# A reordered turn in phase C, and one-hot rows of places that GpSimd makes and DRAM carries over to phase D

## What is computed

```python
x = x + jnp.tanh(g_xattn[2]) * _L2_xattn_ref(_layernorm(x), ctx_1024, ...)   # similarity attention
x = x + jnp.tanh(g_ffn[2])   * _L2_ffn_ref(_layernorm(x), ...)               # small feed-forward
x = x + jnp.tanh(g_xattn[3]) * _L3_xattn_ref(ctx_1024, ctx_1024, _layernorm(x), mask, ...)  # 16 heads of 16
x = x + jnp.tanh(g_ffn[3])   * _L3_ffn_ref(_layernorm(x), ...)               # 32 experts, top 4, and a shared one

def _L3_ffn_ref(x, router_w, router_bias, gate_w, up_w, down_w, sgate_w, sup_w, sdown_w):
    flat = x.reshape(B * T, D)
    scores = _softmax(flat @ router_w.T + router_bias)
    topk_scores, topk_idx = jax.lax.top_k(scores, 4)
    topk_scores = topk_scores / jnp.clip(topk_scores.sum(-1, keepdims=True), 1e-12, None)
    h = silu(einsum('nd,ehd->neh', flat, gate_w)) * einsum('nd,ehd->neh', flat, up_w)
    sel = take_along_axis(einsum('neh,edh->ned', h, down_w), topk_idx[:, :, None], axis=1)
    out = (sel * topk_scores[:, :, None]).sum(axis=1)
    return out + silu(flat @ sgate_w.T) * (flat @ sup_w.T) @ sdown_w.T
```

## Time and profile before

| | us |
|---|---|
| median of 3 runs | 4344.7 |
| profiled execution, whole | 4317.87 |
| its span, first to last instruction | 4316.1 |
| phase C, head attention's turns 0 to 15 | about 2983 to 3780 |
| phase C's last instruction | 3804.6 |
| phase D | 3806 to 4316 |
| a full turn of phase C | 50.55 |

### The profile page before, as it was taken

How to read it: one execution, slowest core, us unless ns; L and a number is a source line. 1 busy time by engine, 2 the same in 40 slices (tenths; PEclk the granted TensorE clock), 3 DMA queues, 4 the chain that set the end, 5 groups by cost and what they waited for, 6 DMA issues and landing times. The chain is left out here.

```text
span 4316.1 us, 78135 instructions
## 1 busy us (share of the span) xinstructions
PE 3976.5 (92%) x29168; PEld 2824.2 (65%) x29168; DVE 2323.2 (54%) x7158; ACT 1772.2 (41%) x3733; POOL 945.7 (22%) x1118
## 2 busy tenths in 40 slices
PE   7999999999999999999998899988999998769996
PEld 4666666666666666666665589966666666438963
DVE  4555655565556655665554522125566666474445
ACT  4455555555555455545542211113444444313420
POOL 2221222122212221222120011111000000005667
PEclk9999999999999999999999999999999999879998
DMA  3000000000000000000000169940000100029964
GB/s 114 1 4 9 8 6 4 9 8 6 3 9 8 6 4 9 8 6 4 6 13 33 74 237 333 332 165 13 30 23 26 31 21 11 13 71 299 335 200 143
DMA packets 136623, 284.25 MB, mean 66 GB/s; under 512 B 19968, under 2 KB 90176, under 8 KB 127680
## 3 DMA queue, kind: packets, MB, share of 16 engines
q1 hardware_dynamic: 84944, 200.03, 13.3%
q0 software_dynamic: 18336, 50.09, 4.0%
q10 hardware_dynamic: 32976, 29.13, 2.0%
HBM read 229.12 MB, written 50.07 MB: 65 GB/s over the span
## 5 line engine op out<-in xcount | busy, mean ns | idle before, releaser
L466 POOL TENSOR_SCALAR a_wide_p<-a_wide_p,a_w_inv 128x512 f32<-128x512 f32 x512 | 355.3, 706 | 1438.8 <-DVE a_w_inv L1133 1438.8
L903 ACT ACTIVATE a_wide_p<-a_wide_p,a_row_min 128x512 f32<-128x512 f32 x512 | 363.4, 713 | 114.0 <-DVE a_row_min L1128 112.5
L1203 DVE TENSOR_REDUCE a_q_pad<-ring 128x4 f32<-128x1024 f32 x256 | 301.1, 1219 | 87.5 <-PE ring L696 87.4
L1128 DVE CUSTOM_DVE_ANT_0 a_wide_p<-ring,a_neg_keys 128x512 f32<-128x512 f32 x403 | 266.0, 688 | 125.0 <-PE ring L550 124.8
L550 PE MATMUL ring<-a_qk 64*128 64x512 f32 x806 | 289.1, 643 | 21.6 <-DVE a_row_min L1128 15.0
L960 ACT ACTIVATE a_probs<-ring 128x1024 f32<-128x1024 f32 x256 | 250.5, 1019 | 72.6 <-PE ring L710 72.6
L1621 PE MATMUL ring<-b_xgt,b_we 128*128 128x128 f32 x2016 | 235.7, 275 | 0.5 <-DVE b_xgt L1784 0.5
L1621 PEld LDWEIGHTS ring<-b_xgt,b_we 128*128 128x128 f32 x2016 | 230.2, 192 | 1.1 <-DVE b_xgt L1784 0.7
L2689 DVE CUSTOM_DVE_ANT_0 c_junk<-ring,c_neg_mask 128x256 f32<-128x256 f32 x512 | 181.4, 420 | 89.3 <-PE ring L2219 89.3
L529 PE MATMUL acc<-a_kv_t,shared_w 128*128 128x512 f32 x392 | 196.0, 623 | 1.2 <-ACT a_kv_t L894 1.2
L1550 POOL DMA_INDIRECT d_xg<-d_rows,d_token_idx x159 | 150.1, 944 | 178.6 <-PE ring L1610 102.3
(11 more groups left out here) (464 smaller groups left out, 8547.3 us busy)
## 6 DMA issues: line engine op xcount, KB each, us to landing
b_we<-in_experts SPq DMA_DIRECT2D x63, 1536.0 KB, 9.3
d_we<-in_experts SPq DMA_DIRECT2D x159, 256.0 KB, 4.6
d_results<-d_yb ACTq DMA_DIRECT2D x159, 128.0 KB
b_results<-b_yb ACTq DMA_DIRECT2D x63, 128.0 KB, 9.0
a_cb<-in_ctx SPq DMA_DIRECT2D x16, 256.0 KB, 2.8
b_turned<-a_heads_t SPq DMA_DIRECT2D x16, 256.0 KB
b_rows<-a_heads SPq DMA_DIRECT2D x16, 256.0 KB
shared_x<-b_turned SPq DMA_DIRECT2D x8, 512.0 KB, 5.7
```

Source lines behind the costliest of these rows:

```text
L466: ins = pool.tensor_scalar(wide_p[:, h % 4, t, :], wide_p[:, h % 4, t, :], w_inv[:, t, h:h + 1], 1.0, ALU.mult, ALU.mult)
L903: ins = act.activation(wide_p[:, h % 4, t, :], wide_p[:, h % 4, t, :], ACT.Exp, scale=-1.0, bias=row_min[:, h, t:t + 1], accum_out=row_sum ...
L1128: dve.tensor_tensor_reduce(wide_p[:, h % 4, t, :], wbank(name), neg_keys[w % 2][:], -0.125, 3.0e38, ALU.add, ALU.min, row_min[:, h, t:t + ...
L1203: dve.tensor_reduce(q_pad[:, :, 2 * i:2 * i + 2, HD].rearrange("p t h -> p h t"), s, AX.X, ALU.max, negate=True).then_inc(nr.taken(name), 1)
```

## The change

It has four parts. (1) Phase C's turn is put in another order: TensorE turns c_x_e first, then c_o_t, then the queries; the logits come ahead of the first group of scores; f_out comes behind the second group, the projections n_project and f_project behind the fourth, and x_context behind the second queries. ScalarE follows and copies c_o_t's second half ahead of the last hidden copy. VectorE does n_values_in at the turn's head (with a wait for the values' last use), and e_apply, e_shares and route_choose ahead of x_products. (2) e_rank writes the places too: a rank's lower seven bits, as the starts of experts are whole multiples of 128. GpSimd makes the eight one-hot rows of an element from them (rows_of_places, in shared_x's free half), and SyncE stores them to DRAM (d_places, 256 KB an element). (3) Phase D loads them into by_place, which has four buffers now; chunks 0 to 3 go ahead of d_wd, the twelve others behind it, and d_we behind them. VectorE makes d_by_block alone. (4) The second half of shared_x is loaded at phase D's start instead of in phase C, and make_pairs takes the pairs element by element, as the stored rows lie.

```diff
@@ phase D: SyncE, TensorE, VectorE
                         if finish:
-                            sp.dma_start(wd[:], w_experts[:, :, WS:WN].rearrange("e p n -> p e n")).then_inc(downs_loaded, 16)
+                            sp.dma_start(xt[1], r.turned[:, :, 512:1024]).then_inc(second_loaded, 16)
+                            for c in range(chunks):
+                                if c >= PR:
+                                    sp.wait_ge(pairs_used, c - PR + 1)
+                                sp.dma_start(by_place[:, c % PR, :, :], r.places[:, c, :, :]).then_inc(places_loaded[c % PR], 16)
+                                if c == PR - 1:
+                                    sp.dma_start(wd[:], w_experts[:, :, WS:WN].rearrange("e p n -> p e n")).then_inc(downs_loaded, 16)
...
                             pe.wait_ge(pairs_made, c + 1)
+                            if finish:
+                                pe.wait_ge(places_loaded[c % PR], 16 * (c // PR + 1))
...
+                                if finish:
+                                    k, t = i // 2, 2 * c + i % 2
+                                else:
+                                    k, t = (PAIR * c + i) // T, (PAIR * c + i) % T
+                                    dve.tensor_scalar(by_place[:, c % PR, i, :], count16[:, 0:P], partf[:, 0, k, t:t + 1], None, ALU.is_equal)
                                 ins = dve.tensor_scalar(by_block[:, c % 2, i, :], count16[:, 0:NB], partf[:, 1, k, t:t + 1], token[:, t:t + 1],
@@ phase C: SyncE
-                                for g in range(2):
-                                    sp.dma_start(xt[g], rd.turned[:, :, 512 * g:512 * g + 512]).then_inc(next_loaded, 16)
+                                sp.dma_start(xt[0], rd.turned[:, :, 0:512]).then_inc(next_loaded, 16)
...
+                            if on(i - 3):
+                                sp.wait_ge(e_place_rows, i - 2)
+                                sp.dma_start(rd.places[:, i - 3, :, :], place_rows[:, (i - 3) % 2, :, :]).then_inc(e_places_stored[(i - 3) % 2], 16)
@@ phase C: GpSimd, at each turn's head
+                            pool.wait_ge(e_placed, b + 1)
+                            if b >= 2:
+                                pool.wait_ge(e_places_stored[b % 2], 16 * (b // 2))
+                            for k in range(4):
+                                for t in range(2):
+                                    ins = pool.tensor_scalar(place_rows[:, b % 2, 2 * k + t, :], count16, place_f[:, b % 2, k, t:t + 1], 0.0,
+                                                             ALU.is_equal, ALU.add)
+                            ins.then_inc(e_place_rows, 1)
@@ phase C: TensorE
+                            if on(n - 2):
+                                e_turn(n - 2)
+                            if on(n - 1):
+                                n_turn_out(n - 1)
                             if on(n):
                                 pe.wait_ge(n_queries, n + 1)
                                 n_turn_queries(("Q", n))
-                            if on(n - 1):
-                                n_turn_out(n - 1)
-                            if on(n - 2):
-                                e_turn(n - 2)
...
                             if on(n - 3):
                                 e_count(n - 3)
+                            if on(n - 2):
+                                e_logits(n - 2)
...
@@ phase C: ScalarE
-                            if on(n - 1):
-                                n_values_out(n - 1, 1)
...
                                 f_hidden(f1, 2)
+                            if on(n):
+                                n_values_out(n, 1)
+                            if on(f1):
                                 f_hidden(f1, 3)
@@ phase C: VectorE, e_rank
+                            if b >= 2:
+                                dve.wait_ge(e_place_rows, b - 1)
+                            link(dve.tensor_copy(place_i[:, 0, :, :], rd.rank[:, :, 2 * b:2 * b + 2]))
+                            link(dve.tensor_scalar(place_i[:, 1, :, :], place_i[:, 0, :, :], P - 1, None, ALU.bitwise_and))
+                            dve.tensor_copy(place_f[:, b % 2, :, :], place_i[:, 1, :, :]).then_inc(e_placed, 1)
```

More of the change, by code:

```diff
@@ L1932, in build @@
                     e_turned_stored = sem(ctx, "c_e_turned_stored")
+                    e_placed = sem(ctx, "c_e_placed")
+                    e_place_rows = sem(ctx, "c_e_place_rows_made")
+                    e_places_stored = [sem(ctx, f"c_e_places_stored{i}") for i in range(2)]
                     n_queries = sem(ctx, "c_n_queries_ready")
```

65 lines of the change are left out of this document (43 added, 22 removed).

## The result

The changed kernel took 4295.06 us (median of four runs, 4291.42 to 4298.69), the kernel before beside it 4344.21 (4340.64 to 4346.62): a ratio of 0.9894, with a 95% interval of 0.9882 to 0.9906. That is 46 us less by the ratio and 49 by the medians. In two later comparisons the ratio was 0.9892 (0.9873 to 0.9911) and 0.9895 (0.9880 to 0.9910), while both kernels ran some 30 us faster there: 4267.6 against 4314.9, and 4267.9 against 4313.0.

The account below looks back on a forecast made before the run. Phase C was taken as bound by TensorE plus its waits, phase D's starting loop by VectorE. Terms: -31 (phase C) + 4 (its end) - 15.5 (phase D's loop) = -42.5, say -43, from 4344.7 to 4302 us; range 4286 to 4327.

Parts of the forecast that it names:

- Full turns: Phase C's twelve full turns, n = 2 to 13: reordering saves 2.2 us each, 26.4 us together.
- The four waits that were to be left: TensorE's idle times in a full turn of phase C: to fall from seven to four, among them 0.65 and 1.2 us.
- The first and the last turns: Phase C's first two turns save 1.5 and 1.9 us, its last two 1.0 and 1.3.
- The 0.9 us more behind the last c_o_t: End of phase C: the last element's c_o_t and heads come 0.9 us later, behind moved rows and logits.
- The end of phase C: Last rank to phase D: GpSimd's uncovered last rows and their store add 4 us, or 7.5 at 0.7 us a row.
- Phase D's loop: Start of phase D: without d_by_place on VectorE, an eighth takes 4.75 us instead of 6.9, saving 15.5 us.
- The 27 us between profile and median: Whole kernel: the median of runs lies 27 us above the profiled execution; the forecast applied its saving to the median.
- A: Phase C's turn: the wait moves to another place, a turn gives 0.7 us instead of 2.2; 4323 us, chance 0.14.
- B: Phase D's loop stays long, d_by_place landing late or TensorE's clock low; all 15.5 us lost, 4318 us, chance 0.10.
- C: Phase C's turns: TensorE packs better, all 4.20 us of waits go, 28 us more saved; 4274 us, chance 0.04.
- D: GpSimd's comparison runs like its power; slower than before from 3.0 us an operation, about 4590 us at 5.4; chance 0.04.
- E: Whole kernel: something unseen eats about all of the gain; 4345 us, chance 0.05.

Follow-up runs that it names:

- Experiment 3: Two runs: the changed kernel with VectorE's work in its old places, 4287.5 us; the kernel before with only VectorE's work in its new places, 4316.5 us.
- experiment 4: The changed kernel with the last of 16 elements' one-hot rows made by VectorE in phase D, GpSimd making the other 15: 4261.4 and 4263.6 us.
- last_by_vector: The changed kernel, but VectorE makes the last element's one-hot rows of places in phase D: ratio to the kernel before 0.9889, then 0.9885.
- vector_old: The changed kernel with VectorE's work put back in its old places in phase C's turn: 4287.5 us, ratio to the kernel before 0.9942.
- logits_in_gap: The changed kernel with TensorE's logits behind the first scores, c_heads' turning behind the second, VectorE reading logits between the first two groups' maxima: 4274.1 us, ratio 0.9909.
- logits_spread: Last element's rows by VectorE; against that, two x_project products before the first scores, the rest, c_heads and logits between first and second scores: 4250.6 us, ratio 0.9863.
- places_only: The kernel before with only GpSimd's rows of places by way of DRAM added, phase C's turn in its old order: 4302.2 us, ratio 0.9980.

## Why the prediction was right

**The total.** -43 was forecast, from 4344.7 to 4302; the runs gave 4295 and, in three comparisons, medians 45 to 49 us apart. The range and the sign held, by the mechanism that was put. That the sum lies within a few us is partly luck: the end of C was priced 3.4 us too low, and a shorter opening of phase C, which was not forecast, and a slightly shorter loop made up for it. Term by term:

- **Full turns, 2.2 us each: right.** 2.34 (50.55 to 48.21). The four waits that were to be left, 0.65, 1.2, 0.23 and one before the mask, are 0.69, 1.17, 0.23 and 0.39. The mask stands 3337.13 - 3312.47 = 24.66 us behind the last hidden block; 24.7 was forecast, 27.0 it was. What carried it was to walk through the turn with two fixed distances: c_o_t to the rank, and 4.17 us between groups of scores. Experiment 3 shows that this needed VectorE's new order as well as that of TensorE and ScalarE; these two were never moved apart, so what ScalarE's earlier copy of c_o_t is worth is not shown.
- **The first and the last turns: a little under.** The 15 turns from the first c_o_t to the last give 30.7 to 31.4 us. The opening of phase C is shorter too: 164.5 to 170.1 us in ten profiles with TensorE's new order, 168.0 to 175.1 in four with the old. Some 1.2 of that is only c_o_t's earlier place within its turn. The rest, about 4 us, is the larger part of what the forecast lacked; its spread is as large, so its size is loose. The 0.9 us more behind the last c_o_t is there (22.7 and 23.1 against 23.6 to 23.8).
- **The end of phase C, +4: mis-sized.** It is +7.4. The step was right in all its pieces but one: 0.6 for the places (0.71 in the trace: the rank is done at 3765.97 + 0.42 = 3766.39, GpSimd's first row starts at 3767.10), then the rows, then 3.8 for the store's landing and phase D's start. The rows took 5.57 us instead of 2.3, as I took the cast of the same shape, 283 ns, for the comparison, which measured 700 to 713. 8 x 0.42 = 3.4 (0.70 less 0.28) is the whole error. The other bound, the multiply's 706, was the right one, though by chance: it is of four times as many elements. The text had that case at 7.5.
- **Phase D's loop, -15.5: right.** 70.2 to 52.8 in two profiles and 54.4 in a third, -16 to -17. Blocks stand 4.62 to 4.75 us apart where 4.75 was forecast, and the first two run at the lower level, as the forecast had it; in the third profile that lasted longer (experiment 4). TensorE does not wait on a load once. The issues (KB each, median us to landing, and SyncE's order of time) in the changed kernel:

```profile
d_wd<-in_experts SPq DMA_DIRECT2D x1, 4096.0 KB, 15.7
d_by_place<-d_places SPq DMA_DIRECT2D x6, 256.0 KB, 4.4
```

```profile
3779.07 0.43 SPq L1528 DMA_DIRECT2D d_wd<-in_experts  x1
3794.01 2.17 SPq L1526 DMA_DIRECT2D d_by_place<-d_places  x2
```

  d_wd was in at about 3794.8, and chunk 4's load was issued at 3794.01: so the forecast's claim that the one is through when the other comes missed by 0.8 us, which cost nothing that shows: chunk 4's load landed 2.7 us behind its issue, and the loads behind it took 2.6 to 2.9.
- **The 27 us between profile and median.** I carried it over as a constant. The sum came out, since both timed series of that comparison lie 30 us higher than the later ones; but the profile of before behaves like the later chips (4311.9 to 4314.9), and the first profile of after like its own runs. Taken from the two profiles alone, the gain would read 22 us.

**The rivals.** A (waits elsewhere in the turn) did not happen: turns would be 49.8. B (d_by_place late, or the clock low) did not: from the third on all blocks are 3.64 us long, and TensorE waits for no load. C (TensorE packs fully) did not: 2.48 us of waits are left, for the chain that the forecast named. D asked for 3.0 us a row and found 0.71. E's condition, something unseen that eats the gain, came near in one place: the first profile does have 25 us more in phase D, but not by the change.

The Trainium skill (GPSIMD Engine Reference, Key points) has VectorE about twice as fast for elementwise work, which I had priced at 0.6 us a row. The trace has 0.71 for GpSimd, so the estimate by that page was nearer than the row that I chose. In last_by_vector VectorE starts the next instruction 0.16 us behind such a row (3815.53 to 3815.69, experiment 4), and the row itself lasts 0.25; GpSimd's, which adds a zero besides, start 0.70 apart. By the starts the factor is four here and by the lengths three, not two.

## What to carry to other kernels

Walk through one turn of the loop with the dependent distances and count what stands between them: the places where TensorE's work is shorter than such a distance are where the idle time will be, whatever is moved, and an order of TensorE that VectorE doesn't follow bought less than half here. Work given to an idle engine is free only inside the loop; price the last turn's share and the store behind it by a row of the same operation, or leave the last turn's share with the fast engine. And compare stretches of two profiles, not their spans: here the spans said 22 us and the stretches and timed runs 47.

## What the hardware showed

- A wait of 1.64 us on TensorE at the turn's head was followed by products at the lower clock in 6 of 9 full turns of vector_old (granted clock 0.57 there), one of 1.11 in 2 of 12 turns of logits_in_gap, and the wait of 0.69 in the changed kernel in none. Yet one of 1.27 before the third scores of logits_spread, and one of 1.17 in the changed kernel, left the granted clock at 1.00 (100 us from 3300 on), and the same wait of 1.64 in the 13th turn of places_only and of the kernel before was followed by the lower level at once in the one only. So by these rows the length of one wait alone doesn't decide; what else does is open. A turn with it costs 1.65 to 1.7 us more, and that 13th turn 3.
- GpSimd's comparison of f16 rows against a scalar per partition takes 0.48 us for 64 elements of each partition and 0.71 us for 128, which makes 0.25 us and 3.6 ns an element; a multiply of 512 f32 elements takes the same 0.71.
- ScalarE stood still for up to 24.7 us at a time and VectorE for up to 8.4 in one execution, behind no instruction of the program, while GpSimd issued gathers; in the profiles of the 13 other executions never.
